# Moving the host rows of layer 0 to GpSimd, clearing three lanes of each sum there, and writing the pad term to one lane

## The reference, cut to what matters

```python
def _L0_gnn_ref(x, adj, W1, b1, W2, b2):
    mask = (adj > 0.0).astype(x.dtype)
    W1a, W1b = (W1[:F], W1[F:])
    xj_proj = x @ W1a
    diff = x[:, :, None, :] - x[:, None, :, :]
    h = relu(xj_proj[:, :, None, :] + diff @ W1b + b1)
    hm = jnp.einsum('bjkh,bjk->bjh', h, mask)
    deg = jnp.sum(mask, axis=-1)
    return hm @ W2 + deg[..., None] * b2
# h = jnp.maximum(_layernorm(x, axis=-1), 0.0);  x = x + _L0_gnn_ref(h, adj, ...)
```

## Time and profile before

| | before |
|---|---|
| median of 3 runs | 1501.34 us (1501.23 to 1503.02) |
| the profiled execution | 1501.28 us, span 1499.6 us |
| TensorE (PE) busy | 1331.5 us, 89% |
| VectorE (DVE) busy | 1172.1 us, 78% |
| ScalarE (ACT) busy | 1112.1 us, 74% |
| GpSimd (POOL) busy | 495.7 us, 33% |
| mean granted TensorE clock | 0.97 of full speed |

### The profile page before, as it was taken

One profiled execution on the slowest core, in us unless ns is written; L12 is line 12 of the kernel. 1 busy time (PEld: TensorE's weight loads), 2 busy tenths in 40 slices (PEclk: granted clock), 3 DMA queues, 4 the chain that ended last, 5 costly groups with the idle time before them and its releaser, 6 DMA issues. The chain is left out here.

```text
span 1499.6 us, 41694 instructions
## 1 busy us (share of the span) xinstructions
PE 1331.5 (89%) x11307; PEld 1084.8 (72%) x11308; DVE 1172.1 (78%) x3088; ACT 1112.1 (74%) x2424; POOL 495.7 (33%) x611
## 2 busy tenths in 40 slices
PE   0799999999999999999999999997999997881498
PEld 0577777777777777777777777775889987810498
DVE  6598898988988889889898898885444446968655
ACT  0788888888888888888888888873555555726675
POOL 0143344444444334333444444432111110076300
PEclk9999999999999999999999999998999998976699
DMA  7000000000000000000000000000000000000022
GB/s 148 15 9 9 15 7 7 7 14 7 7 7 10 11 7 7 7 14 7 7 7 14 7 7 7 0 2 1 1 0 0 0 0 0 0 1 0 11 49 52
DMA packets 40749, 18.08 MB, mean 12 GB/s; under 512 B 19396, under 2 KB 40710, under 8 KB 40710
## 3 DMA queue, kind: packets, MB, share of 16 engines
q1 hardware_dynamic: 40178, 17.39, 4.7%
q10 hardware_dynamic: 532, 0.21, 0.1%
HBM read 13.40 MB, written 4.19 MB: 12 GB/s over the span
## 5 line engine op out<-in xcount | busy, mean ns | idle before, releaser
L829 DVE SCALAR_TENSOR_TENSOR acc<-slot_banks,acc 128x768 f32<-128x768 f32 x512 | 486.8, 951 | 44.0 <-PE slot_banks L551 34.0
L897 POOL TENSOR_TENSOR acc<-acc 128x384 f32<-128x384 f32 x128 | 128.1, 1001 | 565.4 <-DVE onediff L823 560.9
L551 PE MATMUL slot_banks<-ac_hi,work 128*128 128x192 f16 x1408 | 264.4, 246 | 1.0 <-ACT slot_banks L715 1.0
L551 PE MATMUL slot_banks<-ac_lo,work 128*128 128x192 f16 x1408 | 263.9, 246 | 0.0
L551 PE MATMUL slot_banks<-ac_hi,onediff 128*128 128x192 f16 x1024 | 186.9, 248 | 20.8 <-DVE acc L829 16.9
L551 PE MATMUL slot_banks<-ac_lo,onediff 128*128 128x192 f16 x1024 | 185.8, 246 | 0.0
L551 PEld LDWEIGHTS slot_banks<-ac_hi,work 128*128 (+1 forms) x1408 | 137.3, 98 | 62.5 <-issue 43.4
L551 PEld LDWEIGHTS slot_banks<-ac_lo,work 128*128 (+1 forms) x1408 | 138.0, 98 | 14.9 <-issue 6.3
L811 DVE TENSOR_SCALAR work<-work,slot_key 128x1024 f16 x256 | 119.6, 478 | 28.6 <-issue 28.6
L551 PEld LDWEIGHTS slot_banks<-ac_hi,onediff 128*128 x1024 | 104.2, 102 | 43.2 <-issue 39.8
L708 ACT ACTIVATE work<-slot_banks 128x576 f32<-128x576 f32 x128 | 83.2, 650 | 68.6 <-PE slot_banks L551 68.6
(11 more groups left out here) (254 smaller groups left out, 3330.3 us busy)
## 6 DMA issues: line engine op xcount, KB each, us to landing
adj_in<-in_adj_dram SPq DMA_DIRECT2D x32, 256.0 KB, 2.8
out_dram<-acc SPq DMA_DIRECT2D x32, 128.0 KB, 2.0
l1w<-in_L_gnn_W_dram SPq DMA_DIRECT2D x2, 64.0 KB
l1b<-in_L_gnn_b_dram SPq DMA_DIRECT2D x2, 64.0 KB
x_all<-in_x_dram SPq DMA_DIRECT2D x4, 0.2 KB, 12.0
nm_in<-in_nodemask_dram ACTq DMA_DIRECT2D x1, 64.0 KB
w1a<-in_L_gnn_W_dram ACTq DMA_DIRECT2D x1, 48.0 KB
w1b<-in_L_gnn_W_dram ACTq DMA_DIRECT2D x1, 48.0 KB
```

The source lines that it names most:

```text
L551: last = nc.tensor.matmul(unit(pair, t, 1), hot(t), part[:, q, H:2 * H].unsqueeze(1), start=False, stop=(e == 1 and (t % SB == SB - 1 or t ...
L829: nc.vector.scalar_tensor_tensor(out=sums, in0=unit((q + k) % 2, 0, SU), scalar=0.0, in1=sums, op0=ALU.min, op1=ALU.add).then_inc(s_free[k ...
L897: nc.gpsimd.tensor_tensor(acc[:, q, 0:2 * H], acc[:, q, 0:2 * H], acc[:, q, 2 * H:4 * H], ALU.add)
```

## The change

Three things.

1. *Host rows.* `dve_from_first`, `dve_past_last` and `dve_host_rows` leave VectorE. `pool_host_rows` on GpSimd does the same nine instructions, and first `shift` (128x4); VectorE hands it `start`, `end` and `first_slot` after `pe_first_rows`. It stands in GpSimd's step of position 2, between `pool_low` and `pool_sum`. ScalarE's `act_rank_nodes` waits for `shift` by a semaphore of its own, `pe_degrees` for `s_first` instead of `s_host`.
2. *Lanes.* `neg_pad` is the whole number of empty slots, ScalarE writes relu(A x neg_pad) to the first lane only (192 columns), and GpSimd clears the other three (`pool_clear`, 576 columns) one graph ahead.
3. *Waits.* VectorE's loop waits for the clearing too (`s_zero`), and GpSimd's step begins with a wait for the transposed sum of the graph that last had these lanes (`s_T`). VectorE's step counter goes by 11 instead of 12.

```diff
         def pe_degrees(pe, g, p):
             pe.wait_ge(s_mask, g + 1)
-            pe.wait_ge(s_host, g)
+            pe.wait_ge(s_first, g)
...
         def act_rank_nodes(act, g):
             act.wait_ge(s_rkT, g + 1)
-            act.wait_ge(s_first, g + 1)
+            act.wait_ge(s_shift, g + 1)
...
-            nc.scalar.activation(acc[:, q, :].rearrange("p (t h) -> p t h", t=SU),
-                                 ac32[:, q, 0:H].unsqueeze(1).broadcast_to([N, SU, H]), ACT.Relu,
+            nc.scalar.activation(acc[:, q, 0:H], ac32[:, q, 0:H], ACT.Relu,
                                  scale=neg_pad[:, p, q:q + 1]).then_inc(s_acc0, 1)
...
-            v.tensor_scalar(neg_pad[:, p, :], pad[:, :], -float(SS - 1), 1.0 / SU, ALU.add, ALU.mult).then_inc(s_n, 1)
+            v.tensor_scalar(neg_pad[:, p, :], pad[:, :], -float(SS - 1), None, ALU.add).then_inc(s_n, 1)
...
-            nc.vector.scalar_tensor_tensor(out=shift[:, :], in0=pSmall[:, 0:GS], scalar=float(SS), in1=own[:, :],
-                                           op0=ALU.mult, op1=ALU.subtract).then_inc(s_first, 1)
-        def dve_from_first(dve, g, p):
-            dve.wait_ge(s_first, g + 1)
-            for q in range(GS):
-                nc.vector.tensor_scalar(host[:, p, q * N:(q + 1) * N], row16[:, :], start[:, q:q + 1], None, ALU.is_ge)
-        def dve_past_last(dve, g):
-            for q in range(GS):
-                last = nc.vector.tensor_scalar(past[:, q * N:(q + 1) * N], row16[:, :], end[:, q:q + 1], None, ALU.is_ge)
-            last.then_inc(s_nop, 1)
-        def dve_host_rows(dve, g, p):
-            dve.wait_ge(s_nop, 12 * g + 12)
-            nc.vector.tensor_tensor(host[:, p, :], host[:, p, :], past, ALU.subtract).then_inc(s_host, 1)
+            nc.vector.tensor_scalar(first_slot[:, :], pSmall[:, 0:GS], float(SS), None, ALU.mult).then_inc(s_first, 1)
...
             dve.wait_ge(s_acc0, b + 1)
+            dve.wait_ge(s_zero, b + 1)
...
+        def pool_clear(q):
+            nc.gpsimd.memset(acc[:, q, H:SU * H], 0.0).then_inc(s_zero, 1)
+
+        def pool_host_rows(pool, g, p):
+            v = nc.gpsimd
+            pool.wait_ge(s_first, g + 1)
+            v.tensor_tensor(shift[:, :], first_slot[:, :], own[:, :], ALU.subtract).then_inc(s_shift, 1)
+            for q in range(GS):
+                cols = slice(q * N, (q + 1) * N)
+                v.tensor_scalar(host[:, p, cols], row16[:, :], start[:, q:q + 1], None, ALU.is_ge)
+                last = v.tensor_scalar(past[:, cols], row16[:, :], end[:, q:q + 1], None, ALU.is_ge)
+            last.then_inc(s_edges, 1)
+            pool.wait_ge(s_edges, g + 1)
+            v.tensor_tensor(host[:, p, :], host[:, p, :], past, ALU.subtract).then_inc(s_host, 1)
...
+                pool_clear(0)
                 pool_low(pool, 0, 0)
                 pool_low(pool, 1, 1)
+                pool_host_rows(pool, 0, 0)
                 def step(b, g, u, q, nxt, p, use):
+                    if not (known(b) and (b < 3 or b + 1 >= B)):
+                        pool.wait_ge(s_T, b - 2)
                     if not (known(b) and b + 2 >= B):
                         pool_low(pool, b + 2, (q + 2) % GS)
+                    if not (known(b) and b + 1 >= B):
+                        pool_clear((q + 1) % GS)
+                    if nxt is not None and q == 2:
+                        pool_host_rows(pool, nxt, p)
                     pool_sum(pool, b, g, q, total, first)
```

More of the change, by code:

```diff
@@ L152, in gnn_stack_kernel @@
         shift = sb("shift", [N, GS])
+        first_slot = sb("first_slot", [N, GS])
         chunks = sb("chunks", [1, B], I32)
@@ L398, in gnn_stack_kernel @@
         s_nop = sem("slot_count_step")
+        s_shift = sem("rank_shifts_made")
+        s_edges = sem("host_row_edges_made")
+        s_zero = sem("sum_lanes_cleared")
         s_n = sem("slot_counts_ready")
@@ L729, in dve_rows @@
             v.tensor_scalar(degp[:, :], pSmall[:, 0:GS], float(SS - 1), None, ALU.add).then_inc(s_nop, 1)
-            dve.wait_ge(s_nop, 12 * g + 1)
+            dve.wait_ge(s_nop, 11 * g + 1)
             v.tensor_tensor(over[:, :, :], degp[:, :].unsqueeze(2).broadcast_to([N, GS, NC]),
                             cand[:, :].unsqueeze(1).broadcast_to([N, GS, NC]), ALU.subtract).then_inc(s_nop, 1)
-            dve.wait_ge(s_nop, 12 * g + 2)
+            dve.wait_ge(s_nop, 11 * g + 2)
             v.tensor_scalar(over_i[:, :, :], over[:, :, :], float(SS - 1), float(DIV), ALU.max, ALU.mult)\
              .then_inc(s_nop, 1)
-            dve.wait_ge(s_nop, 12 * g + 3)
+            dve.wait_ge(s_nop, 11 * g + 3)
             v.tensor_scalar(rows_i[:, :, :], over_i[:, :, :], SH, None, ALU.arith_shift_right).then_inc(s_nop, 1)
-            dve.wait_ge(s_nop, 12 * g + 4)
+            dve.wait_ge(s_nop, 11 * g + 4)
             v.tensor_copy(rows_or[:, :, :], rows_i[:, :, :]).then_inc(s_rows, 1)
@@ L750, in dve_count_full @@
             v = nc.vector
-            dve.wait_ge(s_nop, 12 * g + 5)
+            dve.wait_ge(s_nop, 11 * g + 5)
             v.tensor_reduce(nfull[:, :], over[:, :, :], AX.X, ALU.add).then_inc(s_nop, 1)
@@ L756, in dve_own @@
             v = nc.vector
-            dve.wait_ge(s_nop, 12 * g + 6)
+            dve.wait_ge(s_nop, 11 * g + 6)
             v.tensor_scalar(chunks[:, ds(g * GS, GS)], nfull[0:1, :], 1.0, None, ALU.add)
@@ L764, in dve_left @@
             v = nc.vector
-            dve.wait_ge(s_nop, 12 * g + 7)
+            dve.wait_ge(s_nop, 11 * g + 7)
             v.tensor_tensor(left[:, :], degp[:, :], own[:, :], ALU.subtract).then_inc(s_nop, 1)
@@ L770, in dve_pieces @@
             v = nc.vector
-            dve.wait_ge(s_nop, 12 * g + 8)
+            dve.wait_ge(s_nop, 11 * g + 8)
             v.tensor_scalar(left_i[:, :], left[:, :], float(SS - 1), float(DIV), ALU.max, ALU.mult).then_inc(s_nop, 1)
-            dve.wait_ge(s_nop, 12 * g + 9)
+            dve.wait_ge(s_nop, 11 * g + 9)
             v.tensor_scalar(pieces_i[:, :], left_i[:, :], SH, None, ALU.arith_shift_right).then_inc(s_nop, 1)
-            dve.wait_ge(s_nop, 12 * g + 10)
+            dve.wait_ge(s_nop, 11 * g + 10)
             v.tensor_copy(pieces[:, :], pieces_i[:, :])
@@ L778, in dve_pieces @@
                                    op0=ALU.mult, op1=ALU.add).then_inc(s_nop, 1)
-            dve.wait_ge(s_nop, 12 * g + 11)
-            v.tensor_scalar(neg_pad[:, p, :], pad[:, :], -float(SS - 1), 1.0 / SU, ALU.add, ALU.mult).then_inc(s_n, 1)
+            dve.wait_ge(s_nop, 11 * g + 11)
+            v.tensor_scalar(neg_pad[:, p, :], pad[:, :], -float(SS - 1), None, ALU.add).then_inc(s_n, 1)
         def dve_first_rows(dve, g, p):
@@ L1029, in _ @@
                 dve_first_rows(dve, 0, 0)
-                dve_from_first(dve, 0, 0)
-                dve_past_last(dve, 0)
-                dve_host_rows(dve, 0, 0)
                 dve.wait_ge(s_rs, 1)
@@ L1043, in halfway @@
                             dve_full(dve, nxt)
-                        if nxt is not None and q == 3:
-                            dve_past_last(dve, nxt)
                         if not (known(b) and b < 2):
                             dve_updated_stats(dve, b - 2)
-                        if nxt is not None and q == 3:
-                            dve_host_rows(dve, nxt, p)
                     def middle():
@@ L1070, in late @@
                                 dve_pieces(dve, nxt, p)
-                            if q == 2:
-                                dve_from_first(dve, nxt, p)
                     dve_slots(dve, b, g, u, q, regs, halfway, middle, beside, summed, late)
```

## The result

The changed kernel takes 1638.6 us (median of four runs, 1636.7 to 1640.0) against 1501.8 for the kernel before: 1.091 times as long, interval 1.0894 to 1.0926. The profiled executions differ by as much, spans of 1636.4 and 1499.6 us. The sign was forecast; the size, 1547, was not, and the range ended at 1592.

The account below looks back on a forecast made before the run. Bound: a path alternating between VectorE and TensorE in each group of four graphs. 0.50 + 0.12 + 0.14 + 1.45 - 0.80 = +1.41 us a group, 31 groups +43.7, +2 ahead of the loop: 1547.0 us; range 1490 to 1592.

Parts of the forecast that it names:

- Eight `tensor_scalar`: GpSimd's host rows in q=2: eight instructions of 128 columns take 1.92 us, bounds 1.4 and 3.4.
- my 1.45 us of wait: TensorE's transposes in q=3 start 1.45 us later, behind GpSimd's late pair sum; bounds 0 and +3.0.
- The gain of 0.80: Host rows leaving VectorE in q=3 remove three TensorE pauses: 0.30 + 0.25 + 0.25 = 0.80 us a group.
- The clearing against L817: VectorE's L817 waits for GpSimd's clearing: +0.50 us in q=1, mean +0.12 in q=0, +0.20 for TensorE in q=2.
- The rival by which the clearing blocks nothing: GpSimd's clearing never holds VectorE up: 1486 with host rows in time (chance 0.13), 1528 with rows late (chance 0.15).
- The added wait: One more wait and register step in VectorE's two exposed loop heads: +0.14 us a group, bounds 0 and 0.2.
- VectorE never waits for the clearing: GpSimd makes the clearing a graph ahead, so VectorE never waits for its data; no time was charged.
- Ahead of the loop: The first group's host rows, made before the loop where everything waits for them, cost +2 us on GpSimd.
- ScalarE's shortening: ScalarE's L699 going from 768 to 192 columns gains nothing; bound, if wholly on the path, below 119 us.
- The last rival: GpSimd's `tensor_scalar` costs as much as a two-input instruction: 1.5 us more a group, 1592; chance 0.12.
- slow bound: With slow GpSimd instructions in the host rows, TensorE's transposes in q=3 start up to +3.0 us later.
- second rival: The clearing blocks nothing and GpSimd's rows come in time: 0.14 + 0.10 - 0.80 = -0.56 a group, 1486; chance 0.13.

Follow-up runs that it names:

- e9: The changed kernel with 48 idle matmuls of 128 columns ahead of TensorE's transposes in q=3, filling the wait for GpSimd: 1594.0 us.
- e3: The changed kernel with four of the eight GpSimd `tensor_scalar` left out, so the hosts come out empty: 1515.7 us.
- e6: The kernel before with only `shift` and the four rows past the last made on GpSimd in q=2, lanes as they were: 1476.1 us.
- e8: The kernel before with VectorE's rows past the last and subtraction moved behind the third half of q=3, all still on VectorE: 1496.7 us.
- e1: The kernel before with the lanes' part alone (pad term on one lane, clearing on GpSimd), host rows still on VectorE: 1530.4 us.
- e12: The kernel before with the lanes' part alone, the clearing held back on GpSimd until VectorE's L817 is made: 1507.8 us.
- e13: The kernel before with one more wait in VectorE's loop, on a semaphore met long before: 1504.7 us.
- e2: The changed kernel without the lanes' part: host rows on GpSimd, pad term on four lanes, no clearing: 1621.4 us.

## Why the prediction was wrong

The mechanism that carried the forecast is the one that happened: GpSimd's host rows make the pair sum of q=2 late, and TensorE's transposes in q=3 wait. Two terms were wrong. One of them I had bounded too low, the other was not in the sum at all.

- *Eight `tensor_scalar` (failed, the mis-sized term).* I took 0.24 us from start to start, nearest to the affine select's 293 ns, with 0.47 as the far bound. It is 0.58. An instruction of the same shape was the wrong neighbour: one that does other work costs otherwise per column. With 0.58 the eight alone are 2.7 us longer; VectorE's hold-up, taken at 1.37, was about 0.7 (0.79, 0.76 and 0.91 instead of 0.60). That makes 2.0 more. The rows started 0.3 us sooner than I took, the subtraction was 0.1 shorter, and the rest held. The transposes came 3.1 us late instead of 1.45. That is 1.6 us a group.
- *The clock (failed, a step that was missing).* After 2.9 us without work TensorE ran at 1.2 GHz for a while in most groups: 1.3 to 1.5 us a group, 1.4 by e9, and e3 agrees. At my 1.45 us of wait it would perhaps not have come to that. The traces have single pauses in between: behind 1.75 us (e9, 1077.14) and 1.80 us (e3, 1002.19) the clock stayed at 1.00, behind 2.11 us (e6, 961.48), 2.13 (e8, 974.80) and 2.48 us (the kernel before, 982.44) it fell to 0.50. So the first error probably brought the second with it, but no run has a pause of 1.45 us in every group. The one of the kernel before, with the 3 us behind it:

```profile
982.44 0.25 PE L551 MATMUL slot_banks<-ac_hi,onediff 128*128 128x192 f16 x1 [2.48 <-DVE acc L829]
```

```profile
982.40:985.40 3.00, 2.96 (x20) 2.57 (x21) 3.00 (x10) 0.09 (x1) 2.02 (x4) 0.59 0.00 0
```

- *The gain of 0.80 (held).* e6 gets 0.85 a group; the pauses are gone in the changed kernel too.
- *The clearing against L817 (held in kind, sized too high at each place, and one place forgotten).* 0.30 instead of 0.50 in q=1: L817 ends 0.1 us after GpSimd's instruction, where I had it start then and take its 0.3. Its longest before 1000 us is 783 ns, near the 0.8 us that I named as the sign. Forgotten was L799 in e1; in the changed kernel that instruction is gone. The rival by which the clearing blocks nothing is refuted by e12.
- *The added wait (held within its bounds).* 0.14 was taken; e13 gives 0.1 to 0.2 a group.
- *"VectorE never waits for the clearing" (failed, without a price).* It waits 2.4 us for L875 in every q=0, because the clearing stands behind the late sum. In q=0 VectorE then waits again for TensorE, 2.28 us, so nothing seems to hang on it. This wait is what made the clearing look guilty, and e2 cleared it.
- *Ahead of the loop (too small).* +2 was taken, +5.6 measured: L498 starts at 58.96, L494 did at 53.33, with the same `tensor_scalar` in front of it (eight of them from 52.42 to 57.62).
- *ScalarE's shortening (held: nothing).*

With the two terms put right the sum nearly closes: 1.41 + 1.6 + 1.4 = 4.4 us a group, times 31, and 5.6: 142 us, where the spans differ by 136.8. With 0.30 for q=1 in place of 0.50 it is 136. That it comes so near is in part luck, since the terms of q=0 and of the added wait are known only within bounds. The last rival named the right term, `tensor_scalar` as dear as a two-input instruction, and stopped at 1592, because a two-input instruction is cheaper than this one. The range left out its own slow bound as well: +3.0 in place of +1.45 gives 1595. And the 0.10 in the second rival's sum has no source in the prediction; no run shows that rival's case. The range should have reached further than the dearest row I had for a neighbour: an operation of which the trace has no row is not bounded from above by rows of others.

## What to carry to other kernels

An operation that moves to an engine on which the trace shows none of its kind is to be measured there before anything is built on it: one kernel with a few probes in its setup settled here what the whole forecast hung on. When work goes to an engine with room, add up what stands between its input and the next thing that others need of that engine, not its busy share: GpSimd was at 41% and still too late, while half of the same work (e6) fitted and gave 1.8%. And price a pause of TensorE twice when it gets long, once as waiting and once as slow work behind it. The second price is to be read from many rounds: in this kernel it was 0 in some and 3 us in others, behind waits of the same length.

## What the runs showed of the hardware

- GpSimd's f16 `tensor_scalar` takes 0.45, 0.60 and 1.56 us for 64, 128 and 512 columns; a 512-column subtraction with a broadcast operand 1.04, a clearing of 576 columns 0.58.
- A GpSimd clearing, which reads nothing, holds VectorE's f16 `tensor_scalar` up as a reading instruction does: 0.61 for 0.31 us.
- It is not one-sided. VectorE's L797, which starts 0.18 us after an L885, takes its usual time (two of them in 0.89 us from 569.75), and it is L885 that stretches, from 0.60 to 0.79. Beside L888, of which only 0.3 us were left, L803 took 0.42. By the exclusive lock that the prediction names, L797 would have waited for L885; in this trace it did not. What decides there, I haven't tested.
- TensorE without work for 2.9 us once in about 35 us fell to 1.2 GHz behind 24 of 29 such waits (about 3 us in 20 of them, about 6 in 4) and stayed at 2.4 GHz behind 5; with 48 small matmuls in the pause it stayed at 2.4. A wait of 0.45 us at the same place (e3) left it alone. In e2, where the wait is 2.8 to 3.1 us, all 29 in the trace were followed by the low clock.
- A semaphore wait that is met long before costs VectorE 0.07 to 0.2 us in the loop heads ahead of q=1 and q=2, where L811 waits for "issue": 0.47 and 0.61 us in e13, 0.40 and 0.41 before.
